# The lower halves of a bias for keys 128 to 159 move from an identity pass of their own into spare rows of another pass

## What is computed

```python
def attention(z):                      # z: layer norm of x over the last axis
    bias = einsum('bijd,dh->bhij', z, Wb)
    q, k, v = (einsum('brjd,de->brje', z, W) for W in (Wq, Wk, Wv))   # 4 heads of 32
    sim = einsum('brihe,brjhe->brhij', q, k) * 32 ** -0.5 + bias[:, None]
    sim = where(mask, sim, -1e9)
    o = einsum('brhij,brjhe->brihe', softmax(sim), v)
    return (o * sigmoid(z @ Wg)) @ Wo
x = x + attention(layernorm(x))
t = layernorm(x)
p = softmax(t @ router_w + router_b)   # the 2 largest of 8, scaled to sum 1
x = x + sum over the two of p_e * (t @ expert_w[e] + expert_b[e])
```

## Time and profile before

| | |
|---|---|
| median of 3 runs | 945.65 us |
| lowest and highest | 943.13, 945.79 |
| profiled execution | 944.0, with a span of 941.9 |
| PE busy | 823.1 (87%), 15528 matmuls |
| PE weight load busy | 536.0 (57%) |
| DVE busy | 780.6 (83%), 1813 instructions |
| ACT busy | 485.2 (52%) |
| POOL busy | 641.3 (68%) |
| granted clock, mean of the span | 0.976 |

### The profile page before, as it was taken

One profiled execution on the slowest core, in us unless ns is written; L12 is line 12 of the kernel. 1 busy time (PEld: TensorE's weight loads), 2 busy tenths in 40 slices (PEclk: granted clock), 3 DMA queues, 4 the chain that ended last, 5 costly groups with the idle time before them and its releaser, 6 DMA issues.

```text
span 941.9 us, 40888 instructions
## 1 busy us (share of the span) xinstructions
PE 823.1 (87%) x15528; PEld 536.0 (57%) x15528; DVE 780.6 (83%) x1813; ACT 485.2 (52%) x1049; POOL 641.3 (68%) x1029
## 2 busy tenths in 40 slices
PE   2999689999989999899999899998999989999743
PEld 1897256565655656556566565565655655555421
DVE  8997436888888888888888888888888888888764
ACT  4886145545555455454555545555545555455410
POOL 6993003677776777767777677776777766777777
PEclk9999999999999999999999999999999999999975
DMA  4563000101001010011100011000110001000000
GB/s 133 184 201 121 8 16 24 44 31 38 31 31 43 34 35 28 28 37 40 35 28 28 28 48 35 28 28 28 49 35 28 28 28 47 30 29 24 16 15 15
DMA packets 32460, 40.82 MB, mean 43 GB/s; under 512 B 6288, under 2 KB 27280, under 8 KB 32400
## 3 DMA queue, kind: packets, MB, share of 16 engines
q1 hardware_dynamic: 31920, 39.95, 12.9%
q10 hardware_dynamic: 480, 0.02, 0.0%
HBM read 13.74 MB, written 6.55 MB: 22 GB/s over the span
## 4 chain that ended last, share of the span: by engine, by line
PE 45%; DVE 29%; issue 15%; POOL 7%; ACT 2%; DVEq 0%; DMA 0%; POOLq 0%; ACTq 0%
PE psS L1102 7%; DVE negm L818 6%; DVE rinv L834 5%; PE psS L1077 5%; PE ps_o L1159 3%; POOL ln_s L375 3%; DVE rt L895 3%; PE ps_x L1159 2%; PE ps_o L1162 2%; PE ps_x L1162 2%; DVE rt L898 2%; DVE q_lo L772 2%; POOL xn L378 2%; PE psS L1109 2%; DVE rt L892 2%
## 5 line engine op out<-in xcount | busy, mean ns | idle before, releaser
L428 POOL TENSOR_TENSOR add<-prod 128x256 f32<-128x256 f32 x160 | 116.0, 725 | 101.1 <-DVE prod L936 101.1
L818 DVE TENSOR_REDUCE negm<-psS 128x12 f16<-128x1920 f32 x80 | 145.9, 1823 | 12.6 <-PE psS L1087 8.2
L375 POOL TENSOR_TENSOR ln_s<-ln_s,half 128x5 f32<-128x5 f32 (+1 forms) x60 | 86.1, 1435 | 38.9 <-DVE ln_s L874 31.0
L410 POOL TENSOR_TENSOR rinv_lo<-rinv,rinv_hi 128x160 f16<-128x160 f32 x40 | 19.7, 493 | 115.0 <-ACT rinv_hi L576 115.0
L433 POOL TENSOR_TENSOR add<-add 128x128 f32<-128x128 f32 x200 | 91.2, 456 | 0.1
L545 ACT ACTIVATE pt_b<-psS 128x1920 f32<-128x1920 f32 x40 | 70.8, 1770 | 30.9 <-PE psS L1121 30.9
L601 ACT ACTIVATE hl<-xn 128x320 f16<-128x320 f32 x40 | 18.8, 470 | 129.5 <-POOL xn L378 129.5
L435 POOL TENSOR_TENSOR ymix<-add 128x64 f32<-128x64 f32 x200 | 64.7, 324 | 15.7
L1077 PE MATMUL psS<-bm,ident 128*128 128x480 f16 (+1 forms) x320 | 68.4, 336 | 7.4 <-ACT pt_a L545 3.3
L416 POOL TENSOR_TENSOR og_lo<-og,og_hi 128x320 f16<-128x320 f32 x80 | 62.4, 799 | 17.6 <-ACT og_hi L582 17.6
L1225 PE MATMUL ps_m<-w_hi,og_hi 128*128 128x64 f16 x200 | 28.1, 208 | 51.3 <-DVE rinv L834 46.1
(11 more groups left out here) (274 smaller groups left out, 3028.9 us busy)
## 6 DMA issues: line engine op xcount, KB each, us to landing
xin<-in_x SPq DMA_DIRECT2D x20, 320.0 KB, 2.9
xs_all<-xs_pair SPq DMA_DIRECT2D x20, 320.0 KB, 2.5
xs_q<-xs_all SPq DMA_DIRECT2D x40, 160.0 KB, 2.1
xs_v<-xs_all SPq DMA_DIRECT2D x40, 160.0 KB, 2.1
xin<-in_x SPq DMA_DIRECT2D x40, 160.0 KB, 2.2
out<-res SPq DMA_DIRECT2D x40, 160.0 KB, 1.9
w_raw<-in_expert_w SPq DMA_DIRECT2D x2, 128.0 KB
eb_raw<-in_expert_b SPq DMA_DIRECT2D x15, 2.0 KB
```

The lines of the kernel that those rows point to most:

```text
L375: pool.tensor_tensor(ln_s[a][:, 3, 0:w], ln_s[a][:, 2, 0:w], half[:, 0:w], ALU.pow).then_inc(own, 1)
L428: pool.tensor_tensor(add1[t % 2][:], prod_of(t)[:, 0:4, :], prod_of(t)[:, 4:8, :], ALU.add).then_inc(mix_step[t], 1)
L818: dve.tensor_reduce(negm[c][:, :, 0:slots], psS[:, :, 0:slots * N].rearrange("i h (s j) -> i h s j", s=slots), AX.X, ALU.max, negate=True) ...
```

## The change

- `bt3_lo` has two slots, not three. In `scores` the pass over `bt3_lo` is 320 columns wide for c = 1 too; that over `bt3_hi` stays 480.
- The lower halves for the stacked keys lie in `negm` and `am`, columns 4 to 19 of each head (SHARE = 16 columns in each of the two tiles for c = 0 and 1, together 32 keys). They go through the transpose into `m_t` with the maxima.
- `pick_rest[0]` and `pick_rest[1]` get the rows that pick them: in `mask_tables` two additions on DVE of a piece of `fold` (128 x 64 elements each).
- In `turn_bias_end` the four matmuls of 160 columns become eight of 32 columns (one pair a head), which leave the lower halves with queries on the partitions; the one conversion on DVE becomes four copies of 16 columns a head, two of them on 32 partitions.

```diff
-        bt3_lo = sb("bt3_lo", [P, H, 3, N], F16)
+        bt3_lo = sb("bt3_lo", [P, H, 2, N], F16)
@@ mask_tables
+                rows = fold[:, 4:4 + SHARE].unsqueeze(1).broadcast_to([P, RG, SHARE])
+                part = lambda v, u: v[:].rearrange("p (r j) -> p r j", r=RG)[:, :, SHARE * u:SHARE * u + SHARE]
+                prep_all(dve.tensor_tensor(part(pick_f, 0), part(pick_f, 0), rows, ALU.add),
+                         dve.tensor_tensor(part(pick_rest[1], 1), part(pick_rest[1], 1), rows, ALU.add))
@@ end of the bias, DVE
-                     dve.tensor_copy(bt3_lo[:, :, 2, :], psS[:, :, 0:N]))
+                     *[dve.tensor_copy(negm[u][:, :, 4:4 + SHARE], low_rows(P, 0, u)) for u in range(2)],
+                     *[dve.tensor_copy(am[0:REST, u, :, 4:4 + SHARE], low_rows(REST, 1, u)) for u in range(2)])
@@ turn_bias_end
                 for h in range(H):
-                    mm(psS[:, h, 0:N], lhsT=every, rhs=side_lo[:, h, :], start=True, stop=True)
+                    cols = slice(REST * h, REST * h + REST)
+                    mm(psS[:, 0, cols], lhsT=side_lo[:, h, 0:P], rhs=fold16[:], start=True, stop=True)
+                    mm(psS[0:REST, 1, cols], lhsT=side_lo[:, h, P:N], rhs=fold16[:], start=True, stop=True)
@@ scores
-                for part in (bt3_hi, bt3_lo):
+                for part, wide in ((bt3_hi, slots * N), (bt3_lo, 2 * N)):
                     for h in range(H):
-                        mm(psS[:, h, 0:slots * N], lhsT=ident16[:], rhs=part[:, h].rearrange("j s i -> j (s i)")[:, 0:slots * N],
+                        mm(psS[:, h, 0:wide], lhsT=ident16[:], rhs=part[:, h].rearrange("j s i -> j (s i)")[:, 0:wide],
                            start=part is bt3_hi, stop=False)
```

More of the change, by code:

```diff
@@ L32 @@
 KEPT = (2,)
+SHARE = REST // 2
 WEIGHED = [t for t in range(T) if t not in KEPT]
@@ L805, in _ @@
             dve.wait_ge(bias_turn, 2)
+            low_rows = lambda n, h, u: psS[0:n, h, 0:H * REST].rearrange("i (h j) -> i h j", h=H)[:, :, SHARE * u:SHARE * u + SHARE]
             prep_all(dve.tensor_tensor(bm3[:, :, 2, :], psS[:, :, 2 * N:3 * N], pen[:].unsqueeze(1).broadcast_to([P, H, N]), ALU.add),
```

## The result

| | before | after |
|---|---|---|
| median | 945.18 us (4 runs) | 910.31 us (4 runs, 909.17 to 911.06) |
| ratio, 95% interval | | 0.9637, 0.9624 to 0.965 |
| profiled execution, span | 944.0, 941.9 | 911.06, 909.2 |

The change takes 3.6%, 34.9 us.

The account below looks back on a forecast made before the run. A loop through POOL's string, with rinv at base's end, was taken as the bound. Rounds 29.6 plus start 1.0 make 30.6 less than the profiled 944.0, 913.4; plus 1.65 to the median, 915.0 us; range 912.5 to 944.

Parts of the forecast that it names:

- The second loop through POOL: Steady loop: rinv to POOL's L375 to base to rinv, never passing the shortened call, closes last; mean round 19.73 us.
- The replay against POOL's string: Steady round: DVE 0.27 us earlier waits for one POOL operation less; rinv 0.82 earlier, new round 18.86.
- The margin: DVE's L891 must start before POOL's L435: +0.07 down to -0.03 us to spare, positive in three of four combinations.
- The size of the round: 34 steady rounds shortened from 19.73 to 18.86 us: 29.6 us less if all pass.
- The start: Before the rinv at 162.83: first pass gains 0.5 us, two more rounds 0.27 each, together 1.0 less.
- the preparation: Before the loop, paid once: additions +0.3, matmuls -0.1, conversion -0.2 us; sum 0, from -0.6 to +1.0.
- The end: Last rounds: POOL's own work closes the end, so 0; the low end of the range lets two rounds gain 1.7 us.
- From the profiled execution to the median: Whole kernel: the median of the runs, 945.65, lies 1.65 us above the profiled 944.0, added to 913.4.
- (a): Rival, the pin holds: L891 misses its gap in nearly every round; 2.7 us less, 943.0; chance 0.25.
- (b): Rival, mixed: about half the steady rounds pass; 16 us less, 929; chance 0.15.
- (c): Rival, one for one: POOL's holds shift along and the 0.27 us a round arrives; 935; chance 0.07.
- (d): Rival, slower: DVE is caught at c_stack by POOL's L428, every round 19.84; 949.4 us; chance 0.08.

Follow-up runs that it names:

- e6: The kernel before with POOL's last operation, base, cut to one of 64 columns of a token, PE and DVE unchanged: 922.3 us, ratio 0.9775.
- e5: The changed kernel with 4 x 160 columns put back on PE in the bt3_hi pass of scores(n, 0): 910.5 us, ratio 0.9653.
- e1: The kernel before with only the bt3_lo pass of scores(n, 1) cut from 480 to 320 columns, without the new preparation: 918.6 us, ratio 0.9721.
- e2: The kernel before with the bt3_lo pass of scores(n, 1) cut by 80 columns a head, without the new preparation: 936.2 us, ratio 0.9918.
- e4: The kernel before with the bt3_lo pass of scores(n, 1) cut by 320 columns a head, without the new preparation: 908.6 us, ratio 0.9635.
- e3: The kernel before with the bt3_lo pass of scores(n, 1) cut by 120 columns a head, without the new preparation: 924.0 us, ratio 0.9795.

## Where the prediction was right, and where it failed

**What failed.** The mechanism and the step of the round came out. What failed are terms of the sum. The largest is the 1.65 us that I added to come from the profiled execution to the median: in the changed kernel it measured -0.75, so 2.4 us of the miss of 4.7 lie there. Nearly all of the other 2.3 are in the span: the rounds gained 1.5 more than their term, and the end, put at 0, gained 2.6; the start went the other way, forecast at -1.0 and measured at +1.0. The terms one by one:

**The second loop through POOL, and that it closes last.** Right. e6 shows it, and e5 that PE's amount of work is no bound.

**The replay against POOL's string.** Right to hundredths. Forecast for the changed round: L891 0.20 long, rinv 0.82 earlier, base beside rinv, round 18.86. Measured 0.20, base beginning as rinv starts, 18.82. Three times the cut came back, since one POOL operation less is waited for.

**The margin.** I gave +0.07 to -0.03, positive in three of four combinations of an early or late og and an early or late half of DVE. Those values are right: 0.08 and 0.04 ahead in the changed kernel, and 0.02 behind in e1, where both are late. How often they come was not foreseen: the late og, which half the rounds of the kernel before had, is missing from the steady rounds of the changed kernel. So that all its rounds pass, and not 20 of 34 as in e1, was luck: the four matmuls that go with it were in the diff, but not in my reasons.

**The size of the round.** 34 x (19.73 - 18.82) = 31.1 instead of 29.6, 1.5 us too little: the forecast round of 18.86 was 0.04 longer than the measured mean.

**The start.** Mis-sized: -1.0 forecast, +1.0 in the profiled execution at the first steady rinv (162.83 to 163.84). Of the preparation I had put the sum at 0; the first row_max came 0.5 later (99.82 to 100.34), and in the five traces with the new preparation it lies at 100.19 to 100.94, in the eight without it at 99.55 to 100.25. The term that was mis-sized is the matmuls: -0.1 forecast, +0.36 measured from the end of L779 to DVE's L806 behind them (1.61 to 1.97). The eight small ones follow one another at 0.14 and not at 0.07. They alternate between two tile forms, which may be why; no run separates it. The conversion gained its 0.2 as forecast. The cut gained its 0.5 in the first pass (1.27 for 1.81 in the earlier trace rows) and 0.27 in each of the two rounds behind it. The rest, 1.5 us, is the pace of PE. In both kernels the matmuls from 97 us on run at the pace of 1.2 GHz, though the granted clock of the profile reads 1.00 there; that ends at 107.3 in the kernel before and at 111.7 in the changed one, so that the pass of 320 columns in the first scores took 0.71 before and 1.27 after, on the same code.

```profile
108.10 0.71 PE L1102 MATMUL psS<-bt_lo,ident 128*128 128x320 f16 x4
```

```profile
109.10 1.27 PE L1113 MATMUL psS<-bt_lo,ident 128*128 128x320 f16 x4
```

With the preparation of before, this first rinv lay at 161.5 in e1, 163.8 in e2 (which has the slow pass too) and 161.2 in e4, so 2 to 3 us of the start belong to no change, and one profile can't size this term.

**The end.** Forecast 0, in the low end 1.7; measured 2.6. The three rounds behind the steady ones took 20.53, 19.62 and 17.31 before and take 18.78, 18.80 and 16.47, 3.4 less; what follows them is 0.8 longer.

**From the profiled execution to the median.** The 1.65 was the distance of one profiled execution from the median of three runs, and no property of the kernel. With a fourth run the median of before was 945.18, and its later sets lie at 943.2 to 943.4, below the profiled 944.0. In the changed kernel the profiled execution lies 0.75 above its own median. The range held nothing for this, and it alone is as large as the 2.2 us by which the time lies below it.

**The rivals.** (a), (b), (c) and (d) didn't come about in the changed kernel. (b) is what e3 and e1 are, 924 and 919 against 929. The pin of (a) is seen in e2, with half the cut. (c), one for one, is refuted by the stair.

## What to carry to other kernels

When DVE and GpSimd both run strings of small operations, compare the ends of the longer DVE operations with the ends of GpSimd's: a constant few hundredths between them, as the 0.05 to 0.06 us here, point to GpSimd timing DVE. Then replay the edit against GpSimd's string; the answer is a step and not a slope, and a gain can be several times the cut or nothing. Give the range an allowance for the step from one profiled execution to the median, and doubt any gain whose margin is of the size of shifts that come and go between rounds and executions.

## What was unexpected of the hardware

Between DVE and POOL a few ns decide who holds whom: L891 went through when it started up to 4 ns behind POOL's L435, and then L435 took 0.38 for 0.32; from 6 ns on it was held and took 0.37 for 0.20.

The same PE instructions start 0.05 us later in some rounds than in others (0.29 against 0.24 from max_scores to attend), and with four more matmuls far ahead of them the late rounds were gone. Through the lock between DVE and POOL this was worth 9 us of 919. Its cause is open.

Early in the kernel PE's matmuls take the time of the lower clock level while the granted clock reads 1.00, and the stretch ended at different matmuls in kernels whose code is equal up to there: four of 320 columns in 0.71 in e1 and in 1.27 us in e2.
